# Conditioned low-rank layer: the first operand's products made chunk by chunk, four sums of A moved to VectorE

## What is computed

```
y = einsum('bct,bcd->bdt', x, weights[condition])
scores = y @ Wr.T
gates = softmax(top 16 of 64 scores), zero elsewhere
h = einsum('nd,krd->nkr', y, A)
out = x + 2 * einsum('nkr,kdr->nd', h * gates, B)
```

## Time and profile before

| what | us |
|---|---|
| median of three runs | 718.9 (718.88 to 719.8) |
| the profiled execution's own time | 720.04 |
| its span, first to last instruction | 718.2 |
| time around the span | 1.8 |
| PE busy in the span | 713.1 (99%) |
| DVE, ACT, POOL busy | 480.0, 262.4, 37.1 |

### The profile page before, as it was taken

One profiled execution on the slowest core, in us unless ns is written; L12 is line 12 of the kernel. 1 busy time (PEld: TensorE's weight loads), 2 busy tenths in 40 slices (PEclk: granted clock), 3 DMA queues, 4 the chain that ended last, 5 costly groups with the idle time before them and its releaser, 6 DMA issues.

```text
span 718.2 us, 9247 instructions
## 1 busy us (share of the span) xinstructions
PE 713.1 (99%) x3444; PEld 600.4 (84%) x3444; DVE 480.0 (67%) x937; ACT 262.4 (37%) x499; POOL 37.1 (5%) x30
## 2 busy tenths in 40 slices
PE   9999999999999999999999999999999999999998
PEld 8888888888888888888888888888888888888886
DVE  4798999996536696845343868774534297788552
ACT  5567763534425442133321643121232264223200
POOL 1864000000000000000000000000000000000000
PEclk9999999999999999999999999999999999999999
DMA  9958489856886767475767675855767787545663
GB/s 327 406 177 351 146 307 384 300 219 226 307 312 211 301 230 269 164 246 202 265 247 265 242 297 169 290 175 206 274 223 245 254 303 270 187 147 197 227 222 146
DMA packets 56158, 178.41 MB, mean 248 GB/s; under 512 B 9650, under 2 KB 9778, under 8 KB 55602
## 3 DMA queue, kind: packets, MB, share of 16 engines
q1 hardware_dynamic: 54386, 174.09, 66.9%
q10 hardware_dynamic: 1728, 3.74, 1.4%
HBM read 131.66 MB, written 46.14 MB: 248 GB/s over the span
## 4 chain that ended last, share of the span: by engine, by line
PE 97%; DVE 2%; ACT 0%; issue 0%; POOL 0%; POOLq 0%
PE Pb L267 42%; PE Pb L249 42%; PE Cb L229 7%; PE S L283 4%; PE T L522 1%; DVE Op L182 1%; PE T L300 0%; PE T L355 0%; DVE Wt L200 0%; DVE Op L545 0%; PE Cb L535 0%; DVE Q L365 0%; ACT Op L543 0%; ACT R L235 0%; POOL sS L476 0%
## 5 line engine op out<-in xcount | busy, mean ns | idle before, releaser
L249 PE MATMUL Pb<-Op,Wt 128*128 128x512 f32 x1008 | 238.3, 392 | 0.6 <-DVE Op L545 0.5
L249 PEld LDWEIGHTS Pb<-Op,Wt 128*128 128x128 f32 x1008 | 187.6, 188 | 39.5 <-DVE Op L545 0.6
L267 PE MATMUL Pb<-Wt,Op 128*128 128x512 f32 x912 | 212.1, 391 | 0.0
L267 PEld LDWEIGHTS Pb<-Wt,Op 128*128 128x128 f32 x912 | 170.0, 188 | 34.7 <-DVE Op L182 0.2
L365 DVE TENSOR_TENSOR Q<-Pb,Q 128x512 f32<-128x512 f32 x112 | 77.3, 690 | 91.0 <-PE Pb L267 90.8
L267 PE MATMUL Pb<-Wt,Ox 128*128 128x512 f32 x432 | 100.8, 391 | 0.0
L267 PEld LDWEIGHTS Pb<-Wt,Ox 128*128 128x128 f32 x432 | 80.5, 188 | 16.3
L235 ACT COPY R<-Cb 128x512 f32<-128x512 f32 x60 | 35.2, 588 | 159.6 <-PE Cb L229 159.6
L182 DVE TENSOR_TENSOR Op<-R,Op 128x512 fp32r<-128x512 f32 x98 | 70.1, 740 | 19.0 <-ACT Op L180 19.0
L365 DVE TENSOR_TENSOR Cq<-Pb,Cq 128x512 f32<-128x512 f32 x64 | 44.0, 688 | 49.6 <-ACT Cq L376 30.9
L249 PE MATMUL Pb<-Ox,Wt 128*128 128x512 f32 x288 | 66.3, 389 | 0.0
(11 more groups left out here) (88 smaller groups left out, 455.5 us busy)
## 6 DMA issues: line engine op xcount, KB each, us to landing
Wt<-Wd SPq DMA_DIRECT2D x168, 512.0 KB, 4.8
Wd<-Wt SPq DMA_DIRECT2D x56, 512.0 KB, 4.5
Q<-in_x SPq DMA_DIRECT2D x32, 512.0 KB, 5.0
xc<-in_x SPq DMA_DIRECT2D x24, 512.0 KB, 4.2
out<-Q SPq DMA_DIRECT2D x32, 256.0 KB, 2.6
out<-Q SPq DMA_DIRECT2D x16, 512.0 KB, 2.9
BR<-in_B SPq DMA_DIRECT2D x3, 1024.0 KB, 8.8
BR<-in_x SPq DMA_DIRECT2D x11, 256.0 KB, 11.3
```

Source lines behind the costliest of these rows:

```text
L249: t = pe.run(lambda e, c=c, o=o, a=a, z=z: e.matmul(Pb[:, b, :], Wt[:, k, a, 128 * c:128 * c + 128], part(o, z), start=fresh and (c, a, z) ...
L267: t = pe.run(lambda e, c=c, o=o, k=k, a=a, z=z: e.matmul(Pb[:, b, :], part(o, a)[:, 128 * i:128 * i + 128], Wt[:, k, z, :], start=fresh an ...
```

## The change

It has two parts, both in round 0. First, the first operand is made in another order: the outer loop is over the four chunks `c`, the inner one over the four x tiles `i`, and each bank holds one chunk of all tiles instead of one tile of all chunks. So one bank is one operand, split by `operand` as everywhere else. Unit (0, 0) follows the first operand, unit (0, 1) all four, unit (0, 2) the second copy to `R`. The 6 filling matmuls are gone and there are 22 warming ones instead of 20. Every product of this stage signals, instead of each fourth. Second, the four sums S1 of A go from POOL to DVE, at another place: none in block (0, 0), columns 0 and 1 in block (0, 1), 2 in (0, 2) and 3 in (0, 3), each directly behind unit (1, j) and ahead of the `y11` operands of the same block.

```
--- before.py
+++ after.py
@@ -15,8 +15,7 @@
 NW = 9
 NO = 8
 UNITS = 56
-WARM = 20
-FILL = 6
+WARM = 22
 SPREAD = [1, 3, 4, 7, 16, 18, 20, 22]
 SENT = -3.4028234663852886e38
 
@@ -528,33 +527,22 @@
 
         cond_first(0, cn, t_wa, z_w)
         banks = [Cb[:, 0, :], Cb[:, 1, :], S[:, :], T[:, :, :].rearrange("p a n -> p (a n)")]
-        turns, parts = [], []
-        for i in range(4):
-            pe.after(wbd_ready[i], x0_ready[i][1])
-            for c in range(4):
-                t = pe.run(lambda e, c=c, i=i: e.matmul(banks[i][:, 128 * c:128 * c + 128],
-                                                        x0[i][:, 512 + 128 * c:640 + 128 * c], wbd[:, i, :],
-                                                        start=True, stop=True), c == 3)
-            wbd_free[i] = t
-            turns.append(t)
-            whole = banks[i].rearrange("p (c n) -> p c n", n=128)
-            up, low = [Op[:, 0:4, a, 128 * i:128 * i + 128] for a in range(2)]
-            ac.after(t)
-            hi = ac.run(lambda e, up=up, whole=whole: e.copy(up, whole))
-            ve.after(hi)
-            parts.append(ve.run(lambda e, up=up, low=low, whole=whole: e.tensor_tensor(low, whole, f(up),
-                                                                                       ALU.subtract)))
-            if i == 0 or i == 2:
-                a_unit(0, i // 2, an_ready[i // 2][1])
-        for i in range(FILL):
-            pe.run(lambda e: e.matmul(Pb[:, 3, 0:128], sS[:, 0:128], sS[:, 0:128], start=True, stop=True), False)
-        ops = [(op_spare.popleft(), parts[3]) for c in range(4)]
-        for i in range(4):
-            ac.after(parts[i])
-            R_ready[0][1] = ac.run(lambda e, i=i: e.copy(R[:, 0, 4:8, 128 * i:128 * i + 128],
-                                                         banks[i].rearrange("p (c n) -> p c n", n=128)))
-            (cb_free[0], cb_free[1], s_free, t_free)[i][0] = R_ready[0][1]
-            if i == 0:
+        ops = []
+        for c in range(4):
+            for i in range(4):
+                pe.after(wbd_ready[i], x0_ready[i][1])
+                wbd_free[i] = pe.run(lambda e, c=c, i=i: e.matmul(
+                    banks[c][:, 128 * i:128 * i + 128], x0[i][:, 512 + 128 * c:640 + 128 * c], wbd[:, i, :],
+                    start=True, stop=True))
+            ops.append(operand(banks[c], wbd_free[3]))
+            if c == 0:
+                a_unit(0, 0, an_ready[0][1])
+        a_unit(0, 1, an_ready[1][1])
+        for c in range(4):
+            ac.after(ops[c][1])
+            R_ready[0][1] = ac.run(lambda e, c=c: e.copy(R[:, 0, 4 + c, :], banks[c]))
+            (cb_free[0], cb_free[1], s_free, t_free)[c][0] = R_ready[0][1]
+            if c == 1:
                 a_unit(0, 2, an_ready[2][1])
         op_free[NO + 4] = cond_first(1)
         a_unit(0, 3, an_ready[3][1])
@@ -634,7 +622,9 @@
                         S1 = Cq[:, 2, j, :]
                         if m == 0:
                             a_unit(1, j, an_ready[j][0])
-                            raw["S1", j] = add(gp, S1, A21, A22, an_ready[4 + j][0])
+                            for k in ((), (0, 1), (2,), (3,))[j]:
+                                raw["S1", k] = add(ve, Cq[:, 2, k, :], Q[:, k + 4, 0:512], Q[:, k + 4, 512:],
+                                                   an_ready[4 + k][0])
                         elif m == 1:
                             a_unit(2, j, raw["S1", j])
                             raw["S3", j] = add(gp, A21, A11, A21, raw["S1", j], an_ready[j][0], op=ALU.subtract)
```

## The result

The changed kernel takes **723.17 us** (median of 7 runs, 721.27 to 724.17) beside 718.9 for the kernel before (7 runs, 718.3 to 719.8): slower by 0.55% (ratio over the runs 1.0055, 95% interval 1.0044 to 1.0066; the brackets behind the ratios below are such intervals too). The forecast was 720.7, slower, with a range up to 721.9: the direction came as forecast, the time lies outside.

What follows compares the result with a forecast made beforehand. TensorE bounds the kernel, through its start and DVE's road to the last y11 remainder. Gains of 1.52 + 0.4 us ahead are lost there with 1.77 more: 718.9 + 1.77 = 720.7, own range 719.8 to 721.1, wider range 718.5 to 721.9.

Steps and rivals of the forecast that it cites:

- The start: TensorE's way to block (0, 0): it begins at 12.68 instead of 14.20, 1.52 us earlier, with no gap left for fillers.
- Sums 0 and 1, and POOL's start: S1 of columns 0 and 1 on idle DVE at 20.7 and 21.3, costing nothing; POOL may start at 21.4, not 24.78.
- The road: DVE's instructions to the last y11 remainder: eight instead of six, mostly 1.69 us apart, ending at 38.2 instead of 36.46.
- 1.77: Net loss at the road's end: the last y11 remainder ends 1.77 us later, added to the median 718.9.
- The clock: TensorE's clock behind the waits around block (1, 0): no cost in the sum, a lower level only in a rival.
- Behind the road I cost nothing: After the last y11 remainder: TensorE is later by 1.8, POOL ends sooner, and no further cost is added.
- the stand: TensorE standing idle around block (1, 0), waiting for DVE's remainders: some 2.5 us and 1.0 us.
- the third rival: The stand around block (1, 0) brings back the half clock, costing 2.9 us more: 723.6; chance 0.07.
- its 2.9: Third rival's cost behind block (1, 0): 5.84 us of work at half pace, as long as at the start.
- The share of the order: The new order alone: road of six instructions ending at 35.1, a gain of 1.4 us.
- the other rivals: On DVE's road: no turns, 717.0 (0.12); sums at their own price, 718.7 (0.14). At the start: no lead, 721.9 (0.05).
- its turn: On the road DVE and POOL alternate when both read SBUF, so DVE instructions start 1.69 us apart instead of 0.60.

Runs made afterwards that it cites:

- e1_order_alone: The changed kernel's new order of the first operand, with the four sums S1 on POOL as in the kernel before: 719.63 us, ratio 1.0000.
- e9_sums_behind: The changed kernel, with S1 of columns 2 and 3 on DVE behind the last y11 remainder: 717.71 us, ratio 0.9975.
- e12_fill_second: The changed kernel, with 4 filling matmuls in the second, shorter wait of block (1, 0) only: 722.98 us, ratio 1.0048.
- e5: The changed kernel, with all four S1 on DVE in block (0, 1): 718.14 us, ratio 0.9983.
- e10: The changed kernel, with S1 of columns 0 and 1 on DVE and those of 2 and 3 on POOL: 718.69 us, ratio 0.9990.

## Why the prediction was wrong

**The start**: right. Block (0, 0) was forecast at 12.68 and began at 12.08 (the clock rose about a microsecond earlier in this execution: 44 warming instructions took 7.2 us, 1.32 to 8.54, and the 40 of the kernel before 7.3); no gap behind the products, and no wait of note on the fourth x tile. That last was chance in part: in three other profiled runs of the new order TensorE was early and did wait for that tile, 0.76 us (e1_order_alone), 0.49 (e9_sums_behind) and 0.39 (e12_fill_second), though block (0, 0) still began at 12.06 to 12.43 there.

**Sums 0 and 1, and POOL's start**: right: 20.19 and 21.02, forecast 20.7 and 21.4.

**The road**: right. Unit (1, 2) ended at 25.89, forecast 26.4; the sums took 1.75 and 1.78; the road ended at 37.72, forecast 38.2. Where the clock stays up this is the loss: the kernel with both waits filled lies 1.9 above the kernel before, forecast 1.77. But the size is known only roughly, as the kernel before moves: with the long wait alone filled it is 2.6, and the two runs of the first measurement at clock 1.000, 721.27 and 721.36, are 2.4 above 718.9. The forecast put its 1.77 on that median although the profiled execution, from which it was worked out, was 1.1 longer; so 720.7 was 0.6 too low even for a run without a fall.

**The clock**: here the forecast failed. "Behind the road I cost nothing" was the step: the sum put the clock behind the stand at nothing, and left it to the third rival with a chance of 0.07. Beside that chance stands only that no row of the kernel before shows such a stand; but the same text had forecast the stand, 2.5 us and 1.0 us, and a stretch unlike any in the trace is no ground for a small chance. Measured, 9 of 12 runs have the fall, at 2.7 us in the first profile and 1.4 in the second, and the range ended 1.3 short of the median. The rival had the mechanism and the place. That its time came so near (723.6, the median 723.17) is luck in part: its 2.9 took the lower level to last as long as at the start, and the two profiles show it for 6.8 and 3.4 us. The Trainium skill ("TensorE: Matmul & The Clock Gate", Why this matters for your kernels) warns of idle gaps between bursts of matmuls, which was the rival's rule. The gap that it warns of is longer than the 2.45 us that were enough here, so for this size the measurement decides; that idle time is the cause the runs bear out: with the long wait filled the clock stays, in 13 of 13.

**The share of the order**: wrong in the working, though not in the sum. The gain of 1.4 for the order alone took POOL's and DVE's turns to matter only behind 24.8; e1_order_alone measured no gain. POOL's first two S1 take turns as well, at 15.1 and 18.7, and as soon as TensorE has its lead they decide when the scores begin. In the kernel before they cost TensorE no wait, since it came to the scores about two us later. Moving those two sums was what the order needed (the profiles of e5, e9 and e10 have no wait there); moving the other two ahead of the remainders was the loss.

**What stood against the other rivals** held: no instruction on the road escaped its turn. The Trainium skill's 691 ns ("VectorE: DVE Perf Modes", The TRN2 errata) is right with POOL at rest (0.69); beside POOL the same instruction took 1.75 to 1.78, a case of which that section says nothing. The Trainium skill's page "SBUF — State Buffer" (Who interferes with whom) says that a DVE instruction with two SBUF inputs contends with a GpSimd instruction that reads SBUF. The kernel with POOL held back agrees: 0.69 for the same eight instructions.

Open: why 3 of 12 runs of the changed kernel keep the clock through the same stand, and why the fall is longer in one run than in another; why, with POOL held back, three of six runs show a mean clock of 0.997 and are no longer than the others (721.83 to 722.04 beside 721.69 to 722.36); and what makes the kernel before spread from 718.2 to 720.1.

## What to carry to other kernels

When two engines take turns on memory, price a moved instruction by the turn it takes where it will stand, and look for the place where the engine idles: with the same two sums ahead of remainders that TensorE waits for, the kernel was 1.9 us or more above the one before (clock kept up), and with them behind those remainders 1.8 below. A wait that you forecast for TensorE can have a second price, the clock behind it: here waits of 1.1 and 0.7 us cost no clock in nine runs, and one of 2.45 did in 12 of 17. Where no trace shows TensorE to get through such a wait at full clock, don't give that price a small chance, and test it by filling the wait with matmuls on zeros. An edit that gains time ahead brings forward the next thing that was just in time, so the lead has to be followed into each later wait, by every engine's timetable and not only that of the road you watch.

## What was not expected of the hardware

That matmuls on zeros could speed up a kernel bound by TensorE: 14 of them in the wait brought the changed kernel from 0.45 to 0.55% above the kernel before down to 0.28%, since the clock stayed up behind them. And that the fall has more than one length: 6.8 us at 1.2 GHz in the first profile of the changed kernel, and 3.4 in the second, so that it costs 2.7 or 1.4 us.
